# Moving GpSimd's additions of put-aside results and its fetches of first results to earlier tiles in a routed feed-forward kernel

## The chip, the cores and the metric

One core of one Trainium2 chip runs the whole kernel. The metric is the device time of one execution in microseconds (us), lower is better.

## The reference

Two batches of 2048 tokens with 512 features pass through two layers. Only what shapes the kernel is kept here.

```python
x = x + xattn(layernorm(x), ctx_1024, ctx_1024, mask, ...)   # relu projections, 128 keys per batch,
                                                              # relu scores instead of a softmax
x = x + ffn(layernorm(x), gate_w, Wu, Wv, Wo)

def ffn(x, gate_w, Wu, Wv, Wo):          # 8 experts, inner width 128, the best 2 for each token
    logits = einsum('bnd,de->bne', x, gate_w)
    topv, topi = top_k(logits, 2)
    w = softmax(topv)
    u = einsum('bnd,edr->bner', x, Wu)
    v = einsum('bnd,edr->bner', x, Wv)
    s = silu(u) * v
    Y = einsum('bner,erd->bned', s, Wo)
    return sum over the 2 chosen experts of w * Y
```

Each output row is therefore the attention result, plus a weighted result of the token's first expert, plus a weighted result of its second.

## The kernel before

**First stage.** Sixteen steps of 256 tokens compute attention, the gate and the routing. GpSimd scatters every normalized token twice into `z_dram`, once into the list of its first expert and once into the list of its second. Each row carries the token's number, its weights and what is needed to undo the normalization.

**Second stage.** The lists are cut into 71 tiles of 128 rows (`TILES`). TensorE goes through them in order (`tile_body`, L1717): transpose, up-projection, transpose, down-projection. VectorE weighs the product into the tile's own buffer (`weigh_in`, L1286) and counts up `res_ready`. The buffers form a ring of 20 (`RING`). The kinds of tile are these:

- tiles 0 to 24 (before `FULL`) hold first choices alone, and their result includes the token's own attention row. GpSimd writes them to the output (`store`, L679, DMA at L686, plain).
- tiles 25 to 38 (14 "held" tiles) may hold first and second choices mixed. GpSimd writes the rows that are first results (`store_held`, L702, DMA at L706, plain). SyncE also copies each whole tile to `aside_dram` (`store_aside`, L537), into one of 7 places (`BACK`) when it holds second results.
- tiles 39 to 70 (`FIRST_B` on) hold second choices alone. For 39 to 67, `store` adds the rows to the output, with an accumulating indirect DMA. Before tile 39 it waits until the last twenty stores have landed.
- the last three, 68 to 70 (`SUMMED`), are different: GpSimd fetches the first results of their tokens from the output (`load_firsts`, L691, DMA at L697), VectorE adds them in (L1292, after a wait on `firsts_loaded`), and `store` is a plain one.

**Put-aside results.** SyncE brings the seven put-aside tiles back from `aside_dram` (`load_back`, L546, DMA at L550), and GpSimd adds each to the output (`store_back`, L710, DMA at L713), after a wait on `back_loaded[k]`.

**What sets the order.** The order on GpSimd is written out by hand in the loop at L766, over the tiles t from 25 to 70: the store of tile t first, then any `store_back(k)` with `back_done(k) == t`, then any `load_firsts(a)` with `firsts_wanted(a) == t`. GpSimd carries this list out strictly in order. SyncE has its own list (L565): for each t it copies tile t - 18 aside if that is a held tile, then loads tile t (`load_z`, L516, DMA at L535), then does any `load_back(k)` with `back_wanted(k) == t`. `load_z(t)` waits until the store of tile t - 20 has landed, and if that tile was held, until its copy aside has landed too.

```python
for t in range(FULL, TILES):
    if is_held(t):
        store_held(t)
    else:
        store(t)
    for k in range(BACK):
        if back_done(k) == t:
            store_back(k)
    for a in range(TILES - SUMMED, TILES):
        if firsts_wanted(a) == t:
            load_firsts(a)
```

Of the kernel before, what the change touches and what calls it, by code (L numbers as in the profile page):

```python
# [53 lines left out]
FIRST_B = FULL + 2 * (E - 1)  # L54
HELD = FIRST_B - FULL
TILES = K * NB * TPB + E - 1
# [3 lines left out]
RING = 20  # L60
# [5 lines left out]
SUMMED = 3  # L66
# [39 lines left out]
def moe_block(nc, x, ctx_in, mask, kq, kk, kv, bq, bk, bv, gate_w, Wu, Wv, Wo, out):  # L106
    ctx = ExitStack()
    with ctx:
# [287 lines left out]

        def firsts_wanted(t):

            return FIRST_B + 19 + 3 * (t - TILES + SUMMED)

        def back_wanted(k):

            return FIRST_B + RING + k

        def back_done(k):

            return FIRST_B + 8 + 3 * k

        def x_of(b):

# [28 lines left out]
        def _(sp):  # L439
# [125 lines left out]
            for t in range(TILES):  # L565
                if is_held(t - RING + 2):
                    store_aside(t - RING + 2)
                if t == EARLY:
                    know_tails()
                    sp.wait_ge(head_stored, 16 * E)  # L570
                load_z(t)
                if EARLY <= t < EARLY + E // 2:
                    for e in range(2):
                        copy_tail(2 * (t - EARLY) + e)
                for k in range(BACK):
                    if back_wanted(k) == t:
                        load_back(k)
# [6 lines left out]
        def _(pool):  # L584
# [181 lines left out]
# [11 lines that stand above are left out]
# [1052 lines left out]
```

## Time and profile before

| | us |
|---|---|
| median of 3 runs | 416.85 |
| lowest and highest | 416.48, 417.25 |
| the profiled execution's own time | 416.64 |
| its span | 414.9 |
| TensorE busy | 398.1 (96%) |
| VectorE busy | 331.6 (80%) |
| ScalarE busy | 277.8 (67%) |
| GpSimd busy | 210.3 (51%) |

The span is from the first to the last instruction that the profiler recorded. The execution's own time is 1.74 us longer. Times inside the trace count from the start of the span. GpSimd is POOL in the views, VectorE DVE, TensorE PE, ScalarE ACT, SyncE SP; SPq rows are DMAs that SyncE issued. A DMA's time to landing is from its issue to the arrival of all its bytes.

### The profile page before, as it was taken

How to read it: one execution, taken by the hardware profiler on the slowest of the kernel's cores; microseconds unless marked ns; L12 is line 12 of the kernel's file. 1: busy time of each engine (PE TensorE's matmuls, PEld its weight loads, DVE VectorE, ACT ScalarE, POOL GpSimd, SP SyncE). 2: the span in 40 equal slices, each digit the busy share in tenths (PEclk: the TensorE clock that was granted, in tenths of full speed). 3: DMA queues.
4: the chain of work that ended last, by engine and by line, in shares of the span. 5: the costliest groups of instructions: out<-in, count | busy, mean ns of one | idle time of the engine just before them, and what ended most of it. 6: DMA issues, size and time to landing. Idle time of an engine off the chain costs nothing.

```text
span 414.9 us, 10266 instructions
## 1 busy us (share of the span) xinstructions
PE 398.1 (96%) x3031; PEld 356.1 (86%) x3031; DVE 331.6 (80%) x1108; ACT 277.8 (67%) x596; POOL 210.3 (51%) x227
## 2 busy tenths in 40 slices
PE   8999999999999999999999999999999999999980
PEld 5588899999999999998878988898999999999960
DVE  2678899999999999998787888877887666666760
ACT  1777888888998888888767666666676444444420
POOL 3011125666555565655435545453333567778882
PEclk9999999999999999999999999999999999999995
DMA  7813424677666766443695359779976799997794
GB/s 286 284 65 102 137 92 167 243 256 245 247 233 228 256 212 225 172 164 136 186 315 204 132 187 372 293 267 315 306 237 183 209 242 291 287 248 118 109 108 90
DMA packets 49557, 87.66 MB, mean 211 GB/s; under 512 B 7648, under 2 KB 18400, under 8 KB 49376
## 3 DMA queue, kind: packets, MB, share of 16 engines
q1 hardware_dynamic: 35600, 52.37, 38.9%
q0 software_dynamic: 13904, 34.62, 29.4%
q8 instruction: 28, 0.46, 0.5%
q14 instruction: 25, 0.20, 0.1%
HBM read 44.77 MB, written 48.29 MB: 224 GB/s over the span
## 4 chain that ended last, share of the span: by engine, by line
PE 69%; DVE 15%; issue 5%; ACT 4%; POOL 4%; POOLq 0%; DVEq 0%; ACTq 0%
PE psQ L1547 12%; PE psQ L1548 11%; PE psQ L1549 11%; PE psT L1543 11%; DVE qT L979 2%; PE psO L1547 2%; DVE st L1158 2%; POOL out_dram L686 2%; PE psO L1548 2%; PE psO L1549 2%; PE psZ L1547 2%; PE psZ L1549 2%; PE psZ L1548 2%; PE psQ L1543 2%; PE psS L1547 2%
## 5 line engine op out<-in xcount | busy, mean ns | idle before, releaser
L979 DVE TENSOR_TENSOR qT<-psT,qT 128x512 fp32r<-128x512 f32 x103 | 69.5, 689 | 27.2 <-ACT qT L782 26.8
L629 POOL DMA_INDIRECT z_dram<-zb x64 | 69.3, 1083 | 39.1 <-DVE zb L1267 21.4
L1547 PE MATMUL psQ<-wuv,qT 128*128 x284 | 86.3, 304 | 0.8 <-DVE qT L979 0.4
L1548 PE MATMUL psQ<-wuv,qT 128*128 x284 | 80.2, 283 | 0.0
L1549 PE MATMUL psQ<-wuv,qT 128*128 x284 | 80.1, 282 | 0.0
L1547 PE MATMUL psQ<-qT,wq 128*128 128x256 f32 x256 | 75.2, 294 | 1.5 <-DVE qT L979 1.4
L1549 PE MATMUL psQ<-qT,wq 128*128 128x256 f32 x256 | 72.4, 283 | 0.0
L1548 PE MATMUL psQ<-qT,wq 128*128 128x256 f32 x256 | 72.3, 283 | 0.0
L782 ACT ACTIVATE qT<-psT 128x512 fp32r<-128x512 f32 x103 | 59.4, 593 | 12.1 <-PE psT L1543 12.1
L1547 PEld LDWEIGHTS psQ<-wuv,qT 128*128 128x128 f32 x284 | 53.7, 189 | 5.5 <-issue 1.4
L850 ACT ACTIVATE gate_work<-psQ 128x128 f32<-128x128 f32 x71 | 19.7, 277 | 54.5 <-PE psQ L1549 54.4
L1548 PEld LDWEIGHTS psQ<-wuv,qT 128*128 128x128 f32 x284 | 54.0, 190 | 0.0
L1549 PEld LDWEIGHTS psQ<-wuv,qT 128*128 128x128 f32 x284 | 54.0, 190 | 0.0
L1547 PEld LDWEIGHTS psQ<-qT,wq 128*128 128x128 f32 x256 | 48.9, 191 | 2.4 <-DVE qT L979 2.1
L1548 PEld LDWEIGHTS psQ<-qT,wq 128*128 128x128 f32 x256 | 49.0, 191 | 0.3 <-issue 0.2
L1549 PEld LDWEIGHTS psQ<-qT,wq 128*128 128x128 f32 x256 | 48.9, 191 | 0.0
L686 POOL DMA_INDIRECT out_dram<-wq_flat x24 | 31.3, 1303 | 19.3 <-issue 8.0
L662 POOL TENSOR_TENSOR rstd<-ve,minus_half 128x2 f32<-128x2 f32 x16 | 13.2, 824 | 42.1 <-DVE ve L1166 41.2
L657 POOL TENSOR_TENSOR rstd<-ve,minus_half 128x2 f32<-128x2 f32 x16 | 12.5, 781 | 43.2 <-DVE ve L1166 43.2
L1279 DVE TENSOR_TENSOR gate_work<-gate_work,psQ 128x128 f32<-128x128 f32 x71 | 20.4, 287 | 17.5 <-ACT gate_work L850 16.7
L782 ACT ACTIVATE lgT<-psQ 128x128 fp32r<-128x128 f32 x71 | 19.7, 278 | 19.3 <-PE psQ L1543 18.8
L875 ACT ACTIVATE key_rows<-psQ,bq_sb 128x256 f32<-128x256 f32 x64 | 29.8, 466 | 2.4 <-PE psQ L1549 1.9
(305 smaller groups left out, 1064.6 us busy)
## 6 DMA issues: line engine op xcount, KB each, us to landing
wq_flat<-z_dram SPq DMA_DIRECT2D x28, 264.0 KB, 4.2
xin<-in_x_dram SPq DMA_DIRECT2D x11, 512.0 KB, 3.6
z_dram<-spare SPq DMA_DIRECT2D x17, 264.0 KB, 4.0
qpT_flat<-z_dram SPq DMA_DIRECT2D x11, 264.0 KB, 3.5
zT_ctxT<-in_x_dram SPq DMA_DIRECT2D x5, 512.0 KB, 3.7
kpT_flat<-z_dram SPq DMA_DIRECT2D x9, 264.0 KB, 3.5
vp_flat<-z_dram SPq DMA_DIRECT2D x9, 264.0 KB, 4.1
xn<-z_dram SPq DMA_DIRECT2D x8, 264.0 KB, 4.5
```

The source lines that it names most:

```text
L629: pool.indirect_dma_start(out=z_dram, out_offset=bass.IndirectOffsetOnAxis(ap=z_of(b)[:, t, ROW_COL + k:ROW_COL + k + 1].bitcast(U32), axi ...
L662: nc.gpsimd.tensor_tensor(rstd1[:, :], ve1[:, :], minus_half[:, :], ALU.pow).then_inc(rstd1_ready, 1)
L686: pool.indirect_dma_start(out=out_rows, out_offset=bass.IndirectOffsetOnAxis(ap=zg_of(t)[:, TOK_COL:TOK_COL + 1].bitcast(U32), axis=0), in ...
L782: nc.scalar.activation(o, i, ACT.Copy).then_inc(s, 1)
L850: nc.scalar.activation(sil[:, t % 2, :], psQ[t % 2][:, 0:R], ACT.Silu).then_inc(silu_done, 1)
L875: nc.scalar.activation(tq[:, m % 2, :], psQ[m % 2][:, 0:BT], ACT.Relu, bias=bq_sb[:, m:m + 1]).then_inc(qp_relu, 1)
L979: nc.vector.tensor_tensor(o, a, b, ALU.subtract).then_inc(s, 1)
L1279: nc.vector.tensor_tensor(s_tok[:, t % 2, :], sil[:, t % 2, :], psQ[t % 2][:, R:2 * R], ALU.mult).then_inc(s_ready, 1)
L1543: return pe.transpose(o, i, ident[0:n, 0:n])
L1547: pe.matmul(o, w[LO], a[HI], start=first, stop=False)
L1548: pe.matmul(o, w[HI], a[LO], start=False, stop=False)
L1549: return pe.matmul(o, w[HI], a[HI], start=False, stop=last)
```

## The change

Three small functions give the tile numbers behind which the moved steps stand.

```diff
         def firsts_wanted(t):
-            return FIRST_B + 19 + 3 * (t - TILES + SUMMED)
+            return FIRST_B + 15 + 3 * (t - TILES + SUMMED)
 
         def back_wanted(k):
-            return FIRST_B + RING + k
+            return FIRST_B + RING - 1 + k // 2
 
         def back_done(k):
-            return FIRST_B + 8 + 3 * k
+            return FIRST_B + 3 + 2 * k
```

With `FIRST_B` = 39, `RING` = 20, `TILES` = 71:

| step | engine | before | after |
|---|---|---|---|
| `load_back(0)` to `(6)`, behind `load_z` of | SyncE | 59, 60, 61, 62, 63, 64, 65 | 58, 58, 59, 59, 60, 60, 61 |
| `store_back(0)` to `(6)`, behind the store of | GpSimd | 47, 50, 53, 56, 59, 62, 65 | 42, 44, 46, 48, 50, 52, 54 |
| `load_firsts(68)` to `(70)`, behind the store of | GpSimd | 58, 61, 64 | 54, 57, 60 |

Nothing is added or removed: the number of instructions, of DMAs and of bytes stays the same on every engine.

## Rows read from the trace of the kernel before

**Rows 1.** Chain of work that ended last, its last pieces: start us, us, what.

```profile
376.63 0.67 DVE stage L1296
...
406.80 0.99 POOL out_dram L686
```

**Rows 2.** Timeline of VectorE: start us, us, engine, line, operation, out<-in; tiles 38, 44, 67, 70.

```profile
320.16 0.74 DVE L1305 SCALAR_TENSOR_TENSOR stage<-psO,own,stage 128x512 f32<-128x512 f32 x1
...
336.43 0.74 DVE L1296 TENSOR_SCALAR wq_flat<-psO,wq_flat 128x512 f32<-128x512 f32 x1
...
397.99 0.74 DVE L1296 TENSOR_SCALAR wq_flat<-psZ,wq_flat 128x512 f32<-128x512 f32 x1
...
404.05 0.75 DVE L1292 SCALAR_TENSOR_TENSOR qpT_flat<-psO,qpT_flat,maskT 128x512 f32<-128x512 f32 x1 [0.48 <-PE psO L1549]
```

**Rows 3.** Timeline of GpSimd: stores of tiles 38, 39, 42, 44.

```profile
321.70 0.98 POOL L706 DMA_INDIRECT out_dram<-stage,own_to  x1 [1.70 <-DVE stage L1305]
326.59 1.60 POOL L686 DMA_INDIRECT out_dram<-stage  x1 [3.90 <-DVE xn L1296]
...
332.39 1.56 POOL L686 DMA_INDIRECT out_dram<-wq_flat  x1 [0.46 <-issue]
...
338.67 1.58 POOL L686 DMA_INDIRECT out_dram<-wq_flat  x1 [1.99 <-issue]
```

**Rows 4.** GpSimd's timeline further on: first addition, fetch 68, store 59.

```profile
347.83 1.56 POOL L713 DMA_INDIRECT out_dram<-zb  x1 [0.30 <-issue]
...
377.50 1.08 POOL L697 DMA_INDIRECT x<-out_dram,wq_flat  x1 [0.30 <-DVE stage L1296]
378.88 1.59 POOL L686 DMA_INDIRECT out_dram<-stage  x1 [0.30 <-issue]
```

**Rows 5.** GpSimd's timeline, the end: fetch 70, then stores 67 to 70.

```profile
395.26 1.08 POOL L697 DMA_INDIRECT maskT<-out_dram,qpT_flat  x1 [0.30 <-issue]
...
402.27 1.56 POOL L686 DMA_INDIRECT out_dram<-wq_flat  x1 [0.30 <-issue]
404.13 1.03 POOL L686 DMA_INDIRECT out_dram<-wq_flat  x1 [0.31 <-issue]
405.48 1.02 POOL L686 DMA_INDIRECT out_dram<-qpT_flat  x1 [0.30 <-issue]
406.80 0.99 POOL L686 DMA_INDIRECT out_dram<-qpT_flat  x1 [0.30 <-issue]
```

**Rows 6.** SyncE's queue: last copy aside, loads of tiles 58 and 59, first bring-back.

```profile
333.20 0.35 SPq L544 DMA_DIRECT2D aside_dram<-stage  x1
...
339.21 1.43 SPq L535 DMA_DIRECT2D stage<-z_dram  x2
340.74 0.44 SPq L550 DMA_DIRECT2D zb<-aside_dram  x1
```

**Rows 7.** Time to landing of the last copy aside, issued at 333.20.

```profile
DMA to landing us min/median/max: 4.9/4.9/4.9
```

**Rows 8.** Time to landing of the load of tile 58 (339.21), then the first bring-back (340.74).

```profile
DMA to landing us min/median/max: 3.3/3.3/3.3
DMA to landing us min/median/max: 5.3/5.3/5.3
```

**Rows 9.** Time to landing of store 38 (321.70), all tile loads, all bring-backs.

```profile
DMA to landing us min/median/max: 4.0/4.0/4.0
DMA to landing us min/median/max: 2.6/3.8/13.6
DMA to landing us min/median/max: 5.3/7.7/12.5
```

**Rows 10.** Stretches: length, PE, PEld, DVE, ACT, POOL busy, PE clock, DMA share, GB/s.

```profile
334.50:347.80 13.30, 13.30 (x102) 12.43 (x100) 9.11 (x20) 5.76 (x15) 7.83 (x5) 1.00 1.06 263
347.80:377.50 29.70, 29.70 (x226) 27.77 (x224) 20.26 (x45) 12.83 (x34) 23.42 (x16) 1.00 1.04 247
377.50:404.10 26.60, 25.73 (x182) 22.67 (x180) 17.20 (x39) 10.17 (x28) 22.06 (x15) 1.00 0.85 114
```

## The prediction

> **What bounds the kernel now.** I began with the chain of work that ended last. It runs through TensorE for most of the span, but leaves it near the end: its last compute piece is VectorE's write of tile 59 at 376.63 us, and from there to the last store at 406.80 there is only GpSimd and its issue time [rows 1]. VectorE had the last tile ready at 404.05 + 0.75 = 404.80 [rows 2]. So since 377 us the end has been set by how fast GpSimd works off its list. In its timeline the reader sees one indirect DMA right behind the other, with 0.30 us between them [rows 4, 5]. Store 67 starts at 402.27, though its data was ready at 397.99 + 0.74 = 398.73.
>
> The prices on GpSimd are plain from starts that follow each other. An accumulating store takes 404.13 - 402.27 = 1.86 us, a fetch 378.88 - 377.50 = 1.38, a plain store 1.35 and 1.32, and the last one 0.99 without a follower [rows 4, 5]. Three tiles with one addition cost 4 x 1.86 = 7.4 us, with a fetch as well 8.8 us. TensorE gives three tiles in 8.0 us (tile 44 is ready at 337.17, tile 67 at 398.73 [rows 2]: 61.56 / 23 = 2.68 each). GpSimd falls behind only where fetches are due too.
>
> Spreading the additions forward looks like a gain: if GpSimd were never late, store 70 would start 0.8 us after 404.80. That delay is the one of tile 38, which VectorE had ready at 320.16 + 0.74 = 320.90 [rows 2] and whose store started at 321.70 [rows 3]. The end of GpSimd's work would be 405.6 + 0.99 = 406.6 in place of 407.79, so **at most 1.2 us can be gained**. Whether it is depends on when the first addition can run.
>
> **The change, part by part.** No instruction, DMA or byte is added on any engine; orders change in two queues.
>
> **SyncE.** The first bring-back moves from behind load 59 to behind load 58. What holds load 58 is the last copy aside: issued at 333.20, landed 4.9 us later at 338.1, load 58 issued at 339.21 [rows 6, 7]. `store_aside` of tile 38 is late because each copy waits for the one before it, and nothing that comes before 334 us is changed. The first bring-back was issued at 340.74. Now it directly follows load 58, at about 339.21 + 0.37 = 339.6 (0.37 us is the usual distance between two such issues, the 0.33 of the rows and the register work). The move thus buys 1.1 us, no more. The other six bring-backs also come earlier; six transfers of 264 KB run ahead of tile loads 60 to 65, whose tiles are needed 35 us later. I cost that at nothing: each load has a slack of many tiles, and if it were gone, TensorE would wait in `turn_g`.
>
> **GpSimd.** `store_back(0)` moves from behind store 47 to behind store 42. Store 42 starts at 332.39 [rows 3], so the addition is at the head of the queue at 332.39 + 1.86 = 334.25. Its data is not even requested then: it is issued at 339.6. **GpSimd's queue is in order, so the stores of tiles 43 and on wait behind it.** For the landing the rows give 3.3 us (load 58, just ahead of it) and 5.3 us (this same bring-back before, with additions in flight) [rows 8]. I take 3.8, nearer the lower, since GpSimd issues nothing in the meantime. The outer ends are 2.6 (fastest of the tile loads) and 7.7 (median bring-back) [rows 9]. From landing to the next GpSimd start I take 0.9 us: store 38 landed at 321.70 + 4.0 = 325.70 [rows 3, 9] and store 39, which waited for that, started at 326.59. So GpSimd resumes at T = 339.6 + 3.8 + 0.9 = 344.3, **10.05 us later** than 334.25.
>
> From T on all its data is ready, so it runs its list without a gap. That list has 25 accumulating stores (43 to 67) and 7 additions, 32 x 1.86 = 59.5 us; 3 fetches, 4.1; and the last three stores, 1.35 + 1.32 + 0.99 = 3.7. Together 67.3 us. Before, the same list ran from 334.25 to 407.79, which is 73.5 us, so 6.2 us of it was idle time, waiting for tiles or for room. The stall of 10.05 eats these 6.2 us first, and 3.85 us are left: GpSimd ends at 344.3 + 67.3 = 411.6.
>
> One term is unknown. Store 44 started at 338.67 although its data was there at 336.43 + 0.74 = 337.17 [rows 2, 3]; with the usual 0.8 us it was 0.7 late, put down to issue, in a stretch where the transfer engines are full (share 1.06 [rows 10]). From 348 to 377 they stay so (1.04). After the stall all of GpSimd's traffic runs dense, so I allow between 0 and 1.2 us for such lateness, and take 0.5.
>
> **Fetches.** Fetch 68 now starts at T plus 19 steps of 1.86, at 379.6, later than the 377.50 of before although it stands 4 tiles earlier; fetch 70 starts at about T + 49 = 393.5, against 395.26. VectorE needs the last at 404.05. With any landing up to 9 us it is covered. Fetch 68 also waits for the load of tile 68, which follows the landing of store 48 (starting near 359); some 10 us spare. Cost nothing; if the cover went, VectorE would be late with tiles 68 to 70, but their stores come after 407 anyhow.
>
> **TensorE.** Nothing that it needs gets late. Load 63 waits for store 43, now near 346, and tile 63 is transposed near 380. Its end at 404 stays; the clock stays 1.00 throughout [rows 10].
>
> **Sum.** 3.85 + 0.5 = 4.35 us more. What follows GpSimd's last store (407.79 to the end of the span at 414.9) stays. The profiled execution of 416.64 becomes 421.0. The median is 0.21 above it, so I forecast 421.2.
>
> A rule of the Trainium skill (DMA: Bandwidth & Descriptors, Anatomy of one DMA) gives a transfer about 2.0 us plus its bytes at 436 GB/s. For 264 KB that is an estimate of 2.6 us where the rows show 3.3 and 5.3; by it T would be 343.1 and the sum 3.15 us, still slower.
>
> **The rivals.**
>
> **The first addition is not late (faster or the same).** The place is the wait on `back_loaded[0]`. Break-even is where the stall equals the 6.2 us of idle, a resumption at 340.5; every us earlier gains up to the 1.2 us above, for 415.6. For it speaks that the rest of the list is then well spread. Against it: the bring-back would have to land by 339.6, the time at which I expect its issue. The fastest that I can build is a copy aside landing in 2.6 us like the fastest tile load [rows 9], then 1.1, 0.4, 2.6 and 0.9: 333.20 + 7.6 = 340.8, the break-even itself.
>
> **Stall plus a full transfer path (slower by 6 or more).** After T, 14 tile loads and bring-backs and 12 accumulating DMAs fall into 22 us. Between 377 and 404, with hardly any loads, 15 GpSimd DMAs took a share of 0.85 of 26.6 us, 1.5 us of all engines each [rows 10]. With about 0.55 for a plain load (from the share left of 1.04 in 348 to 377), that is 25.7 us of work in 22, a share of 1.17, above the 1.06 seen. GpSimd would be slowed by up to 2 us more, and with a bring-back of 7.7 us it comes to 416.85 + 4.35 + 2 + 3.9 = 427 at the worst; its middle is 423.5.
>
> **The change does nothing.** If the wait were already met through another order of the semaphores, time stays at 416.9. Nothing speaks for it: the wait is on the bring-back's own semaphore.
>
> **How the numbers follow.** The forecast gets 0.77, the full path 0.18, no change within 0.2% (0.8 us, about what a measurement of this kernel can tell) 0.02, faster 0.03. The low end takes the 2.6 us landing and no lateness: 416.85 + 3.85 - 1.2 = 419.5, and I go to 419.0 for an earlier copy aside. The high end takes a landing of 5.3 (+1.5) and lateness of 1.2 (+0.7) on 421.2, which is 423.4, and reaches to 423.8 for the middle of the rival.
>
> **What would show it.** Right: GpSimd idle from about 334 to 344, released by the bring-back into `zb`; then starts 1.86 us apart with 0.30 between, up to the last near 411; TensorE's end unchanged near 404; 7 us of tail. Wrong: the first `store_back` at 334.3 with no idle before it, a landing of bring-back 0 beyond 6 us, or TensorE idle in the last 60 us.

## The result and the profile after

The change makes the kernel slower: 420.04 us (median of 7 runs, 418.49 to 421.96) against 417.01 us for the kernel before (7 runs, 416.48 to 417.74). The ratio is 1.006, with a 95% interval of 1.0033 to 1.0087 (the quotient of the two medians, 1.0073, is not the same number, and lies inside the interval). The profiled execution took 420.35 us, with a span of 418.6 us; before it was 416.64 and 414.9. The forecast was 421.2, with a range of 419.0 to 423.8.

GpSimd's timeline of the changed kernel, in the places of [rows 3] and [rows 4] (start us, us, engine, line, operation, out<-in, count, idle before it and what ended that):

```profile
322.37 0.98 POOL L706 DMA_INDIRECT out_dram<-stage,own_to  x1 [1.70 <-DVE stage L1305]
326.90 1.60 POOL L686 DMA_INDIRECT out_dram<-stage  x1 [3.55 <-DMA out_dram<-stage,own_to]
...
333.06 1.56 POOL L686 DMA_INDIRECT out_dram<-wq_flat  x1 [0.81 <-DVE wq_flat L1296]
343.88 1.56 POOL L713 DMA_INDIRECT out_dram<-zb  x1 [9.26 <-DVE wq_flat L1296]
345.74 1.58 POOL L686 DMA_INDIRECT out_dram<-wq_flat  x1 [0.30 <-issue]
...
379.36 1.08 POOL L697 DMA_INDIRECT x<-out_dram,wq_flat  x1 [0.30 <-issue]
```

The row at 343.88 is the reading that matters. The first addition starts 10.82 us after store 42, and 9.26 us of that is idle. The profile puts the wait down to VectorE's write of `wq_flat`. But `store_back` has no such wait, and the next such write, that of tile 43, was over at 334.24 + 0.74 = 334.98:

```profile
334.24 0.74 DVE L1296 TENSOR_SCALAR wq_flat<-psZ,wq_flat 128x512 f32<-128x512 f32 x1
```

What came in just ahead of 343.88 is the bring-back, as the next rows show. From the first addition on, every idle time up to the last store is 0.30 or 0.31 us.

SyncE's queue of the changed kernel, against [rows 6]:

```profile
334.05 0.35 SPq L544 DMA_DIRECT2D aside_dram<-stage  x1
...
339.75 0.33 SPq L535 DMA_DIRECT2D stage<-z_dram  x1
340.19 0.85 SPq L550 DMA_DIRECT2D zb<-aside_dram  x2
```

The first bring-back is issued at 340.19, right behind load 58. Its landing took, where [rows 8] has 5.3:

```profile
DMA to landing us min/median/max: 2.9/2.9/2.9
```

So it landed at 343.1, and GpSimd went on 0.8 us later. The end of GpSimd's timeline, against [rows 5]:

```profile
393.39 1.07 POOL L697 DMA_INDIRECT maskT<-out_dram,qpT_flat  x1 [0.30 <-issue]
...
405.99 1.56 POOL L686 DMA_INDIRECT out_dram<-wq_flat  x1 [0.30 <-DVE qpT_flat L1292]
407.85 1.03 POOL L686 DMA_INDIRECT out_dram<-wq_flat  x1 [0.30 <-issue]
...
410.51 0.99 POOL L686 DMA_INDIRECT out_dram<-qpT_flat  x1 [0.30 <-issue]
```

VectorE's last write, which answers to the last of [rows 2], comes 1.04 us later than before, but the last store comes 3.71 us later:

```profile
405.09 0.75 DVE L1292 SCALAR_TENSOR_TENSOR qpT_flat<-psO,qpT_flat,maskT 128x512 f32<-128x512 f32 x1 [0.48 <-PE psO L1549]
```

**Where the time went, by the two profiled executions.** From the head of the queue behind store 42 to the end of the last store:

| | before | after |
|---|---|---|
| head of the queue behind store 42 | 334.25 | 333.06 + 1.86 = 334.92 |
| end of the last store | 407.79 | 411.50 |
| whole stretch | 73.54 | 76.58 |
| the list without any idle (from the changed kernel, 411.50 - 343.88) | 67.62 | 67.62 |
| idle | 5.92 | 8.96 |

The stretch is 3.04 us longer, and the medians differ by 3.03 us. The profiled executions differ by 3.71 us, since this one was already 0.67 us behind at store 42, ahead of anything that was changed.

### The profile page after: what moved, and what is told of

It is laid out like the page before. It is cut to its first block, busy times and chain, and to the rows that moved or that the text cites. A ratio compares the mean times of both kernels' runs of the same rounds, so it can differ in the third digit from the quotient of the medians.

```text
span 418.6 us, 10266 instructions
## 1 busy us (share of the span) xinstructions
PE 398.6 (95%) x3031; PEld 356.7 (85%) x3031; DVE 331.3 (79%) x1108; ACT 277.8 (66%) x596; POOL 210.1 (50%) x227
## 4 chain that ended last, share of the span: by engine, by line
PE 73%; DVE 16%; ACT 4%; issue 2%; DMA 1%; POOL 1%; SPq 0%; POOLq 0%; DVEq 0%; ACTq 0%
PE psQ L1547 12%; PE psQ L1548 12%; PE psQ L1549 12%; PE psT L1543 11%; PE psO L1547 3%; PE psO L1548 2%; PE psO L1549 2%; PE psZ L1547 2%; DVE qT L979 2%; PE psZ L1549 2%; PE psZ L1548 2%; DVE st L1158 2%; PE psQ L1543 2%; PE psS L1547 2%; PE psG L1643 1%
```

## The experiments

**Theory.** GpSimd's list stands still at its first addition until the bring-back has landed. What is lost is this stall, less the idle time that the list had anyhow. **Rivals.** The denser burst of bring-backs and accumulating stores slows the transfers; or the list with additions two tiles apart is too much for GpSimd, whatever its start; or the fetches cost something of their own.

Each ratio is against the kernel before, run beside the experiment. Its median was 417.02 us beside experiments 1, 2, 6 and the first addition behind tile 40 in experiment 8, 417.14 beside 3, 7 and the rest of 8, and 417.49 beside 4, 5 and the two kernels that were run again.

**1. The additions alone.** Bring-backs and fetches as before.

```diff
         def back_done(k):
-            return FIRST_B + 8 + 3 * k
+            return FIRST_B + 3 + 2 * k
```

> Only the additions move (behind tiles 42 to 54); the bring-backs stay behind loads 59 to 65 and the fetches behind 58 to 64. Theory (GpSimd's list stands still until bring-back 0 has landed): the bring-back is issued one load later, about 1.5 us after its 340.2 in the changed kernel, so the first addition starts near 345.4 in place of 343.9, and the rest of the list costs the same 67.6 us. Time 1.5 us above the changed kernel's 420.0, so near 421.5. Rival (it is the dense burst of bring-backs and accumulating stores that slows the transfers): bring-backs one for each load are less dense, so 419.5 or less, with the first addition no later than 344.

Measured: 422.25 us (4 runs, 420.33 to 426.27), ratio 1.015 (1.0097 to 1.0203). The profiled one took 420.33. In its timeline:

```profile
332.03 1.56 POOL L686 DMA_INDIRECT out_dram<-wq_flat  x1 [0.72 <-DVE wq_flat L1296]
343.83 1.56 POOL L713 DMA_INDIRECT out_dram<-zb  x1 [10.24 <-DMA zb<-aside_dram]
```

Here the profile names the bring-back itself as what ended the wait. The stall is 0.98 us longer than the changed kernel's 9.26, where 1.5 was expected. The first addition did not start at 345.4, because load 58 went out 1.47 us earlier in this execution (338.28, against 339.75), and the bring-back with it (339.81). So the start alone, before 344, would fit the rival as well; the time doesn't. GpSimd's last store ends at 411.48, as in the changed kernel (411.50): the additions by themselves bring the whole loss, with the bring-backs as spread out as before.

**2. The bring-backs alone.**

```diff
         def back_wanted(k):
-            return FIRST_B + RING + k
+            return FIRST_B + RING - 1 + k // 2
```

> Only the bring-backs move (behind loads 58 to 61); additions stay behind 47 to 65, fetches behind 58 to 64. Theory: nobody waits for them, and the first addition still starts near 347.8, behind store 47: 417.0, within 0.5 us of the kernel before. Rival (the burst on the transfer engines costs time by itself): slower by 1 us or more, with gaps marked issue in GpSimd's list between 340 and 350.

Measured: 416.39 us (10 runs), ratio 0.9973 (0.9951 to 0.9995). There is no loss from the burst, rather a hint of a gain, a little beyond the 0.5 us that were allowed. Store 44 was held as before (idle of 2.01 us ahead of it, 1.99 in [rows 3]), and it starts at 338.42, before the first bring-back is issued (339.32). So that lateness is not from the bring-backs; what causes it stays open.

**3. The fetches alone.**

```diff
         def firsts_wanted(t):
-            return FIRST_B + 19 + 3 * (t - TILES + SUMMED)
+            return FIRST_B + 15 + 3 * (t - TILES + SUMMED)
```

> Only the three fetches move (behind tiles 54, 57, 60). Theory: GpSimd has 0.57 us of idle left behind tile 54 (before the store of tile 56), and a fetch brought ahead of it fills it: its last store ends 0.5 us earlier, the time is 416.5. The DVE waits for no fetch. Rival (fetches need the transfer engines while they are full, and hold GpSimd up): 417.5 or more.

Measured: 420.68 us (10 runs), ratio 1.0069 (1.0043 to 1.0095). **The expectation was wrong**: this part alone costs as much as the whole change. Its timeline shows a second wait of the same kind:

```profile
365.62 1.56 POOL L686 DMA_INDIRECT out_dram<-kpT_flat  x1 [0.30 <-issue]
371.11 1.08 POOL L697 DMA_INDIRECT x<-out_dram,wq_flat  x1 [3.93 <-DMA wq_flat<-z_dram]
```

`load_firsts(68)` waits until tile 68 itself is loaded, because that tile carries the token numbers. SyncE issued that load at 359.0, and it took

```profile
DMA to landing us min/median/max: 11.3/11.3/11.3
```

so it landed at 370.3, while GpSimd stood ready at 365.62 + 1.86 = 367.5. The time by itself would fit the rival too (an early fetch costs by its own traffic); experiment 4 tests that.

**4. The fetches two tiles later.** The kernel before with fetches behind 56, 59 and 62.

```diff
         def firsts_wanted(t):
-            return FIRST_B + 19 + 3 * (t - TILES + SUMMED)
+            return FIRST_B + 17 + 3 * (t - TILES + SUMMED)
```

> The kernel before with its fetches behind tiles 56, 59, 62, two tiles later than where the change has them. Theory: fetch 68 comes to the head near 371.6 plus the addition behind 56, at 373.5, after the load of tile 68 has landed (370.3), so GpSimd doesn't wait, and the time is 417.0 within 0.5. Rival (an early fetch costs by its own traffic, and not by the wait for the tile's load): still 419 or more.

Measured: 417.36 us (12 runs, 416.47 to 420.51), ratio 1.0007 (0.9989 to 1.0026). The loss is gone, which speaks for the wait for the tile and against the fetch's own traffic. Only the times say so here: the one profile shows 0.30 us ahead of fetch 68, but in it GpSimd reaches the fetch at 377.56, already late, and not near 373.5. That profiled execution was the slowest of the twelve, 420.51, and shows why:

```profile
353.30 1.56 POOL L713 DMA_INDIRECT out_dram<-zb  x1 [6.39 <-DVE qpT_flat L1296]
```

That is the first addition, behind tile 47 as in the kernel before. In this execution the last copy aside was issued only at 338.93 (333.20 in [rows 6]), the bring-back at 345.49, and it took 7.0 us. The wait is there in the old order too, when the chain of copies aside is late. There is little room for that: in the kernel before the bring-back landed at 340.74 + 5.3 = 346.0, so with the usual 0.8 us the addition could start at 346.8, and it started at 347.83. One us was to spare.

**5. The change without its fetches.**

```diff
         def firsts_wanted(t):
-            return FIRST_B + 15 + 3 * (t - TILES + SUMMED)
+            return FIRST_B + 19 + 3 * (t - TILES + SUMMED)
```

> The change with its fetches put back behind tiles 58, 61, 64. Moved alone, the fetches had cost 3.5 us, since GpSimd stood 3.9 us in front of fetch 68 until the load of tile 68 had landed. Theory: in the change this second wait is hidden, because the first stall has already made GpSimd late, and it reaches fetch 68 only at 379; so putting the fetches back changes nothing: the same as the changed kernel within 0.7 us, near 420.0. Rival (the fetches' cost is part of the change's loss): 416.5 to 417.5.

Measured: 420.88 us (6 runs), ratio 1.0079 (1.0048 to 1.011). On the same chip the changed kernel itself, run again, gave 421.05 us (8 runs), ratio 1.0077 (1.0043 to 1.0111):

> The changed kernel once more, unaltered, beside the others on one chip: 420.0 within 0.7, GpSimd's first addition at 344 within 1 us, no other wait in its list.

The time came out a us above what was expected, with the kernel before at 417.49 there, and the first addition started at 345.10, 0.1 us outside what was allowed, after 10.75 us of idle. Every later idle time was 0.30 or 0.31. Putting the fetches back changes nothing: by the medians, the additions cost 5.2 us alone, the fetches 3.5, and the whole change 3.0 in the first measurement and 3.6 in this one. The first stall makes GpSimd so late that tile 68 has landed when it gets to the fetch. In experiment 5 a third wait shows, VectorE's for fetch 70:

```profile
405.86 0.75 DVE L1292 SCALAR_TENSOR_TENSOR qpT_flat<-psO,qpT_flat,maskT 128x512 f32<-128x512 f32 x1 [1.64 <-DMA maskT<-out_dram,qpT_flat]
```

It costs nothing, because the store of tile 70 comes up only at 410.94.

**6. The additions where the change puts them, with data that is there.** The reverse order works because of how the copies aside lie in `aside_dram`. They are not one place for each tile: each copy starts lower than the one before it by as many rows as that one had second results (L1107), so the second results are packed from the end downwards, and what is a first result in a copy is written over by the next. The 14 held tiles have 4096 - 25 x 128 = 896 first results, so any eight of them, 1024 rows, have at least 128 others. Place 7 is therefore final once eight copies have landed, place 6 after nine, and so on. The bring-backs can go in that order, behind loads 51 to 56 and 58.

```diff
         def back_wanted(k):
 
-            return FIRST_B + RING - 1 + k // 2
+            return FULL + RING + 6 + k + k // (BACK - 1)
...
             def load_back(k):
+                sp.wait_ge(aside_stored, 16 * (BACK + k + 1))
                 if k == 0:
-                    sp.wait_ge(aside_stored, 16 * HELD)
                     sp.wait_ge(x1_ready, 2 * NB)
-                sp.dma_start(back[k], aside_dram[(k + 1) * P:(k + 2) * P, :]).then_inc(back_loaded[k], 16)
+                sp.dma_start(back[k], aside_dram[(BACK - k) * P:(BACK - k + 1) * P, :]).then_inc(back_loaded[k], 16)
```

> The additions and fetches stand where the change puts them (behind 42 to 54 and 54 to 60), but the seven bring-backs are issued behind loads 51 to 56 and 58, in the reverse order of places, each as soon as no later copy aside can touch its place. Bring-back 0 should land near 322. Theory: the first addition starts at 334.3 to 335 without a stall, GpSimd's last store ends near 406.6 (0.8 us behind VectorE's last tile), and the time is 415.8, 1.2 us below the kernel before and 4.2 below the changed one. Rival (the list itself is too dense for GpSimd or the transfer engines): at 417 or above although no addition waits.

Measured: 415.71 us (12 runs, 415.2 to 417.12), ratio 0.9962 (0.9943 to 0.9981). The first bring-back was issued at 321.80 and took 3.0 us. Its timeline:

```profile
332.99 1.56 POOL L686 DMA_INDIRECT out_dram<-wq_flat  x1 [0.30 <-issue]
334.85 1.56 POOL L713 DMA_INDIRECT out_dram<-zb  x1 [0.30 <-DVE wq_flat L1296]
...
399.63 1.55 POOL L686 DMA_INDIRECT out_dram<-wq_flat  x1 [1.11 <-DVE wq_flat L1296]
402.13 1.03 POOL L686 DMA_INDIRECT out_dram<-wq_flat  x1 [0.94 <-DVE wq_flat L1292]
404.50 1.02 POOL L686 DMA_INDIRECT out_dram<-qpT_flat  x1 [1.34 <-DVE qpT_flat L1292]
405.82 0.99 POOL L686 DMA_INDIRECT out_dram<-qpT_flat  x1 [0.30 <-issue]
```

The same list, as dense as in the change, now gains. At the end GpSimd waits for VectorE again instead of being late: the last store starts 0.9 us after the last tile (ready at 404.92). This excludes the rival that the list is too dense. The transfer engines had a share of 1.06 between 347.8 and 377.5, against 1.02 in the changed kernel, and GpSimd's steps kept their 1.87 us.

Two things show in this profile besides. The bring-backs now stand between the copies aside in SyncE's list, and the last copy went out at 339.35 and load 58 at 347.23, 6 and 8 us later than before; TensorE did not wait for it. And the fetches had little room: the load of tile 68 was issued at 359.93, no earlier than in experiment 3, and took 8.6 us, so it landed 1.8 us before GpSimd came to fetch 68 at 370.33. Run again:

> The kernel with early bring-backs and the change's list once more: 415.7 within 0.5, below both the kernel before and the changed one; the first addition at once behind store 42, and GpSimd's last store 0.9 us behind VectorE's last tile.

It gave 415.86 us (12 runs), ratio 0.9952 (0.9934 to 0.997), and the load of tile 68 landed 6.0 us before its fetch. **This version beats both kernels.**

**7. Early data with the old list.** As 6, but additions behind 47 to 65 and fetches behind 58 to 64.

```diff
-            return FIRST_B + 15 + 3 * (t - TILES + SUMMED)
+            return FIRST_B + 19 + 3 * (t - TILES + SUMMED)
...
-            return FIRST_B + 3 + 2 * k
+            return FIRST_B + 8 + 3 * k
```

> Early bring-backs as in the kernel that had them behind loads 51 to 58, but GpSimd's list as before the change (additions behind 47 to 65, fetches behind 58 to 64). Theory: nothing waits for the data there, so early data alone gives nothing: 417.0, within 0.5. Rival (early bring-backs themselves relieve the transfer engines and give the gain): 415.8 as with the early list.

Measured: 416.8 us (10 runs), ratio 0.9979 (0.9957 to 1.0002), not told apart from the kernel before. Early data is what makes the early list possible; for itself it gives little or nothing.

**8. The first addition at other tiles.** Behind 40 (alone, the others as in the change), and all seven shifted to begin behind 44 or 45.

```diff
         def back_done(k):
-            return FIRST_B + 3 + 2 * k
+            return FIRST_B + 1 if k == 0 else FIRST_B + 3 + 2 * k
```

> The changed kernel with its first addition behind tile 40 in place of 42, all else as in the change. Theory: bring-back 0 lands when it did, so the first addition starts at the same 343.9, give or take 0.5, and the stores of tiles 41 and 42 now stand behind it: 2 x 1.87 = 3.7 us more than the changed kernel, 423.7. Rival (the loss is in how dense the list is later on, not in what stands behind the first wait): within 0.7 us of the changed kernel's 420.0.

```diff
         def back_done(k):
-            return FIRST_B + 3 + 2 * k
+            return FIRST_B + 5 + 2 * k
```

> The changed kernel with its additions behind tiles 44, 46 to 56. Theory: store 44 ends its step near 340.5, the first addition starts near 344 to 344.8, a stall of about 4; the list behind it is 63.9 us and ends at 407.9 to 408.7, so 416.8 to 417.6, level with the kernel before. Between this and the first addition behind 42 (420.0) and behind 45 lies one store of 1.87 us for each tile, less what the landing moves. Rival (it is density, not the stall): no more than 0.7 us from the changed kernel's 420.0.

```diff
         def back_done(k):
-            return FIRST_B + 3 + 2 * k
+            return FIRST_B + 6 + 2 * k
```

> The changed kernel with its additions behind tiles 45, 47 to 57 in place of 42, 44 to 54; bring-backs and fetches as in the change. Theory: store 45 is done near 342.5, bring-back 0 lands near 344 to 345, so the stall is 1 to 3 us; the list behind it is 3 stores shorter, 62.0 us, and ends at 406.6 to 407.5: 415.7 to 416.6, below the kernel before. Rival (additions two tiles apart are too dense whatever the start): above 417.5.

| first addition behind | median us, runs (lowest, highest) | ratio (95%) | bring-back 0 issued | addition starts | last store ends | list from there |
|---|---|---|---|---|---|---|
| 40 | 422.12, 4 (420.85, 425.55) | 1.013 (1.0081 to 1.0179) | 337.02 | 342.18 | 413.53 | 71.35 |
| 42 (the change) | 420.04, 7 (418.49, 421.96) | 1.006 (1.0033 to 1.0087) | 340.19 | 343.88 | 411.50 | 67.62 |
| 44 | 419.68, 12 (416.89, 421.87) | 1.0032 (1.0001 to 1.0064) | 342.98 | 348.22 | 412.11 | 63.89 |
| 45 | 419.19, 12 (415.77, 422.77) | 1.0013 (0.9979 to 1.0047) | 343.10 | 349.29 | 411.29 | 62.00 |

The lists behind the first addition came out to the step: 71.35 - 67.62 = 3.73 and 67.62 - 63.89 = 3.73 are two stores each, 1.89 is one. What was wrong in the three expectations is the start. It did not stay near 344, but moved from 342.2 to 349.3, and ate most of what a later place gives. **All three times came out wrong**: 422.12 where 423.7 was expected, 419.68 where 416.8 to 417.6, and 419.19 where 415.7 to 416.6. With 44 and 45 the medians even lie where the rival of density had put them. The times alone can't tell the two apart; against density speak the stall in each profile, the list without a gap behind it, and experiment 6. The row behind tile 45:

```profile
349.29 1.56 POOL L713 DMA_INDIRECT out_dram<-zb  x1 [6.94 <-DMA zb<-aside_dram]
```

In these four executions most of the shift is in the issue of the bring-back, 337.02 to 343.10, so 6.1 of 7.1 us. The issue follows the last copy aside. With 45 that copy went out at 336.17, although that kernel is the kernel before, instruction for instruction, up to load 58, and there it was 333.20 [rows 6]. So executions of the same code differ by 3 us there. The copy's own landing differs too: 2.5 us with 40, 4.9 with 42, 4.8 with 44 and 5.7 with 45. The rest is the landing of the bring-back: 4.4, 2.9, 4.5 and 5.4 us, all with GpSimd issuing nothing in the meantime. How much of the shift belongs to the place of the addition, and how much to chance, one profile of each can't tell, and that stays open. The runs spread over 5.0 us with 44, and over 4.9 with 45 without the longest one, 422.77; that would fit a time that follows the landing.

## Why the prediction was right

**What bounds the end.** Right. The last store of the changed kernel ends 3.71 us later while VectorE's last write moves 1.04. With experiment 6 the end went back to 0.9 us behind VectorE.

**SyncE.** Right. I had the first bring-back 7.2 us after store 42 starts (339.6 - 332.39); it was 7.13 (340.19 - 333.06). That it fits so closely is luck: in the other executions with that order of bring-backs and an unchanged list up to store 42 it was 7.23 (experiment 2), 7.43 (5), 8.48 (the change again), 9.27 and 10.14 (first addition behind 45 and 44). I had taken the chain of copies aside as fixed, since nothing ahead of 334 us was changed, and it isn't.

**GpSimd's stall.** Right in kind, a us too long in this profile: 10.05 forecast, 8.96 measured (9.55 in experiment 5, 9.94 in experiment 1 and 10.45 in the change run again). The landing took 2.9 us and not 3.8, and from there to GpSimd's start 0.8 and not 0.9. The bring-back was faster than the neighbour that I leaned on (3.3 us). The rule of the Trainium skill (DMA: Bandwidth & Descriptors, Anatomy of one DMA) gives an estimate of 2.6 us for 264 KB, and the Trainium skill has the rule from DMAs that GpSimd issues. It was nearer here than my 3.8, though this one is SyncE's. Other transfers of that size were far from it, as the 11.3 us of experiment 3 shows.

**The list.** Right. 67.3 us were forecast and 67.62 measured; the old idle time that hides part of the stall was taken as 6.2 and was 5.92.

**Lateness from full transfer engines.** Too high. I allowed 0.5 us of a possible 1.2; the measured value is nothing, every idle time behind the stall being 0.30 or 0.31. With these terms, 8.96 - 5.92 = 3.04 in place of 4.35. That the medians differ by 3.03 is closer than one profile can promise: run again, they differed by 3.56. The forecast for the profiled execution, 421.0, came within 0.7 of the 420.35 partly because that execution was 0.67 us late before the change sets in.

**Fetches.** Right for this kernel, and incomplete. Fetch 68 started at 379.36 (379.6 forecast) without a wait. The load of tile 68 was issued at 366.98 and took 3.8 us, so 8.6 us were to spare, where I had said some 10. But that room is there only because the first stall makes it. In the old list there is none: moved alone, the fetches cost 3.5 us. My sum started from the stalled list, but I never asked what the fetches cost without the stall, not even in the rival where the first addition is on time. Without the first stall this second wait may come next: in experiment 6 GpSimd missed it by 1.8 us, since all seven additions stand ahead of the fetch there and it comes up at 370.33, not at 367.5.

**TensorE.** Right. It waits for no transfer in the last 60 us. Its last matmul ends at 405.05, 1.03 us later than before, of which 0.67 is there at store 42 already; no run explains the other 0.36.

**The rivals.** The low branch, a first addition on time, needs the data by 334: experiment 6 built it, and it gave 415.7, where I had worked out 415.6 as the limit. The full transfer path did not show. That two halves of the change hide each other's cost was in none of my rivals.

## What to carry to other kernels

In a queue that is carried out strictly in order, a step moved forward is free only if what it waits for has landed by its new place; otherwise everything behind it moves back by the stall, less the idle time that the list had. Look up the issue of the transfer that feeds it, then what holds that issue, before moving the consumer. And a part of a change that costs nothing beside the others may still hold a wait of its own, hidden behind the first one: test the parts alone before keeping any.

## What the runs showed of the hardware

- A tile load of 264 KB took 2.6 us at best and 11.3 us in experiment 3, issued at 359.0, where accumulating stores and loads fill the transfer engines (share 1.01 from 347.8 to 377.5 us). A full share alone does not say how long one takes: the load of tile 68 took 3.8 us in the change (share 1.02 in the same stretch), and 8.6 and 5.1 us in the two profiles of experiment 6 (1.06). The first bring-back took 2.9 us in the change, 3.2 in experiment 1, 4.4 behind tile 40, 4.5 behind 44 and 5.4 behind 45, all with GpSimd issuing nothing, and 5.3 before [rows 8].
- GpSimd's step for an accumulating indirect store stayed at 1.56 to 1.59 us, with 0.30 or 0.31 to the next, all through the list behind the stall, at a share of 1.02 of the transfer engines (347.8 to 377.5 us) and at 0.97 (377.5 to 404.1). A plain one took 0.98 to 1.03 us. The issue is not slowed by that load.
- The kernel before has runs up to 421.58 us beside experiments 3, 7 and 8. Experiment 4 caught one long execution with 6.39 us of idle ahead of the first addition, in an order that differs from the kernel before only after tile 56. Of the 90 runs of the kernel before, 29 took more than 418 us. Of the 34 runs with the early bring-backs of experiments 6 and 7 none took more than 417.65, and of the ten of experiment 2 none more than 417.23. That fits a late first bring-back as the cause of the long runs; whether all of them have it was not tested.
